# Scores from two of three half-precision products, and three weight blocks loaded and summed earlier

## The reference

```
style = s @ aff_w.T + aff_b ; w_mod = w * style ; w_mod *= rsqrt(sum(w_mod^2) + eps)
kx = x @ w_mod.T + b                      # per batch element, then 16 heads of 32
A  = softmax(kx[h] . kx[j] / sqrt(32))    # per token, 16 x 16 over its heads
x  = x + modulated_linear(A @ kx)
h = ln(ln(x, pathway), compartment); t = ln(x, time); s = ln(x, scale)
m, n, r = x + _mlp_ln(memory), x + _mlp_ln(noise), x + _mlp_ln(resource)
x  = x + ln(silu(cat(w0 h, w1 t, w2 m, w3 n, w4 r, w5 s) @ W1 + b1) @ W2 + b2)
```

## Time and profile before

| | |
|---|---|
| time, median of 3 | 870.54 us (870.13 to 871.36) |
| the profiled execution: its own time | 869.47 us |
| its span, first to last instruction | 867.6 us |
| PE busy | 836.8 us (96%) |
| DVE busy | 646.7 us (75%) |
| POOL busy | 605.7 us (70%) |
| ACT busy | 487.6 us (56%) |
| mean granted clock of PE | 0.989 of full speed |

### The profile page before, as it was taken

How to read it: one execution, slowest core, us unless ns; L and a number is a source line. 1 busy time by engine, 2 the same in 40 slices (tenths; PEclk the granted TensorE clock), 3 DMA queues, 4 the chain that set the end, 5 groups by cost and what they waited for, 6 DMA issues and landing times.

```text
span 867.6 us, 19685 instructions
## 1 busy us (share of the span) xinstructions
PE 836.8 (96%) x7456; PEld 731.9 (84%) x7474; DVE 646.7 (75%) x1067; ACT 487.6 (56%) x851; POOL 605.7 (70%) x766
## 2 busy tenths in 40 slices
PE   5996999999999999999999999999999999999997
PEld 5853888988889898888989898888988898898986
DVE  3589778778786867678797877679797767677652
ACT  3567555565656465465656556465647546464531
POOL 2367998778786767768776866668787775756472
PEclk9998999999999999999999999999999999999999
DMA  8972233424343333525243332424343342323110
GB/s 277 419 268 62 71 91 105 126 63 150 83 151 81 98 93 86 128 51 158 71 149 89 107 93 69 127 68 145 83 123 91 87 117 49 104 68 83 47 50 25
DMA packets 104365, 95.55 MB, mean 110 GB/s; under 512 B 72880, under 2 KB 78160, under 8 KB 102608
## 3 DMA queue, kind: packets, MB, share of 16 engines
q1 hardware_dynamic: 95056, 69.26, 27.7%
q0 software_dynamic: 4608, 16.78, 7.1%
q10 hardware_dynamic: 4608, 8.25, 2.8%
HBM read 69.60 MB, written 8.40 MB: 90 GB/s over the span
## 4 chain that ended last, share of the span: by engine, by line
PE 88%; DVE 5%; DMA 2%; POOL 2%; issue 1%; ACT 1%; ACTq 0%; another core or an unknown queue 0%; DVEq 0%; POOLq 0%
PE acc L405 43%; PE tok L405 28%; PE att L405 8%; PE xp L558 6%; PE xp L405 3%; DMA kb<-in_kb 1%; DVE stg_e L1284 1%; DMA pgb<-in_pw,pidx 1%; DVE raw_k L1170 0%; DVE W1xl L1274 0%; POOL op0l L1706 0%; DVE qt L1290 0%; POOL W2l L1710 0%; DVE q L1297 0%; DVE BD L1185 0%
## 5 line engine op out<-in xcount | busy, mean ns | idle before, releaser
L1706 POOL TENSOR_TENSOR op1l<-ytmp,op1h 128x512 fp32r<-128x512 f32 x64 | 89.8, 1403 | 20.1 <-ACT op1h L912 19.6
L1652 POOL TENSOR_TENSOR xlo<-xraw,xhi 128x512 fp32r<-128x512 f32 x31 | 40.5, 1306 | 68.0 <-ACT xhi L804 68.0
L405 PE MATMUL acc<-op0h,W1xh 128*128 128x256 f32 x256 | 75.8, 296 | 1.4 <-DVE op0l L1376 1.1
L405 PE MATMUL acc<-op1h,W1th 128*128 128x256 f32 x256 | 75.0, 293 | 0.0
L405 PE MATMUL acc<-op1h,W1hh 128*128 128x256 f32 x256 | 73.7, 288 | 0.0
L405 PE MATMUL acc<-op0h,W1sh 128*128 128x256 f32 x256 | 73.7, 288 | 0.0
L405 PE MATMUL acc<-op1h,W1tl 128*128 128x256 f32 x256 | 72.4, 283 | 0.0
L405 PE MATMUL acc<-op1l,W1hh 128*128 128x256 f32 x256 | 72.4, 283 | 0.0
L405 PE MATMUL acc<-op1l,W1th 128*128 128x256 f32 x256 | 72.4, 283 | 0.0
L405 PE MATMUL acc<-op0h,W1sl 128*128 128x256 f32 x256 | 72.4, 283 | 0.0
L405 PE MATMUL acc<-op1h,W1hl 128*128 128x256 f32 x256 | 72.4, 283 | 0.0
(11 more groups left out here) (269 smaller groups left out, 3005.2 us busy)
## 6 DMA issues: line engine op xcount, KB each, us to landing
xsq<-in_x SPq DMA_DIRECT2D x32, 256.0 KB, 3.1
xb<-in_x SPq DMA_DIRECT2D x32, 256.0 KB, 3.0
out<-xb SPq DMA_DIRECT2D x32, 256.0 KB, 2.4
BD<-q SPq DMA_DIRECT2D x124, 64.0 KB, 2.1
BD<-v SPq DMA_DIRECT2D x124, 64.0 KB
xraw<-in_xT SPq DMA_DIRECT2D x30, 256.0 KB, 3.0
ring<-in_k_wT ACTq DMA_DIRECT2D x6, 256.0 KB, 3.3
dmb<-dm_rows SPq DMA_DIRECT2D x6, 256.0 KB, 3.9
```

Source lines behind the costliest of these rows:

```text
L405: return e.matmul(o, a, b, start=start, stop=True, skip_group_check=True)
L1652: e.tensor_tensor(xlo[:, :, :], (xraw1 if g == 1 else xraw)[:, :, :], xhi[:, :, :].bitcast(F32), ALU.subtract).then_inc(s["xlo"], 1)
L1706: e.tensor_tensor(op[slot]["l"][:, :, half(g)], four(ytmp[YT[n, g][0]]), op[slot]["h"][:, :, half(g)].bitcast(F32), ALU.subtract).then_inc ...
```

## The change

Two things are changed, and a few instructions are placed elsewhere to suit.

First, `scores` leaves out the 32-column matmul (lo weights against hi). By the symmetry of the scores that product is the transpose of the hi.lo product that stands in `SE`. So `score_sum` now makes the transpose of `SE` in 32 x 32 blocks into `ET`, adds `SE` to the hi half, and after that adds `ET`.

Second, in the prologue, the blocks m and n (`raw["x"]`, `stg["a"]`) are loaded right after `o_wT` and r a little later, the blocks t, s, h after the second mlp weights. `mlp1` gets a buffer of its own and runs between `proj(0)` and `demodulation(1)`. `x_scaled`, the Silu of the mlps and `gain_tables` stand ahead of `score_low(0)` on ACT, and `x_weights` stands around `score_sum(0)` on DVE. `tables_tsh` is split, `vec_T` and `tables_mnr` come ahead of `proj(2)`, and `q_hi(2)`, `e_first(1)` stand behind the casts of W1's t block on ACT.

```
             e.dma_start(raw["o"][:, :, :], A["o_wT"]).then_inc(s["c_wo"], 16)
+            e.dma_start(raw["x"][:, :, :], A["int_w1"][2]).then_inc(s["c_rm"], 16)
+            e.dma_start(stg["a"][:, :, :], A["int_w1"][3]).then_inc(s["c_rn"], 16)
             load_sq(1)
-            e.dma_start(stg["a"][:, :, :], A["mlp1"]).then_inc(s["c_m1"], 16)
+            e.dma_start(mlp_w1[:, :, :], A["mlp1"]).then_inc(s["c_m1"], 16)
+            e.dma_start(raw["r"][:, :, :], A["int_w1"][4]).then_inc(s["c_rr"], 16)
...
-                    mm(both, diag(j, 0), q, start=(j % 8 == 0))
-                    i = mm(both[:, :, 0], diag(j, 1), q[:, :, 0])
+                    i = mm(both, diag(j, 0), q, start=(j % 8 == 0))
...
             proj(0)
+            mlp1()
             demodulation(1)
             scores(0)
             proj(1)
             mod_rows(1)
-            mlp1()
-            tables_tsh()
+            mlp2()
+            demod_T()
+            tables_tsh((0,))
             values(0)
-            demod_T()
-            mlp2()
+            tables_tsh((1, 2))
             a_T(0)
             scores(1)
+            tables_tsh((3,))
+            vec_T()
             out_proj(0)
+            tables_mnr()
             proj(2)
-            vec_T()
-            tables_mnr()
             values(1)
...
                 e.wait_ge(s["Sc"], 2 * g + 2)
-                e.tensor_tensor(high, high, SE[:, :], ALU.add).then_inc(s["Ss"], 1)
+                if g:
+                    e.wait_ge(s["aTr"], g)
+                e.transpose(ET[:, :], SE[:, :]).then_inc(s["lT"], 1)
+                e.tensor_tensor(high, high, SE[:, :], ALU.add).then_inc(s["lT"], 1)
+                e.wait_ge(s["lT"], 2 * g + 2)
+                e.tensor_tensor(high, high, ET[:, :], ALU.add).then_inc(s["Ss"], 1)
...
             w_T(0)
+            hidden_add()
             demod_eps(1)
+            x_weights(1, (0, 1))
             score_sum(0)
             less_max(0)
+            x_weights(1, (2, 3))
+            x_weights(2, (0, 1))
             q_lo(1)
             e_T(0)
             q_T(1)
             e_second(0)
-            hidden_add()
+            vectors()
             mod_first(1, range(4))
```

More of the change, by code:

```diff
@@ L136, in build @@
         raw["o"] = raw_o
+        mlp_w1 = at("mlp_w1", [128, 4, 512], offset=place["W2l"])
         stg = {n: at(f"stg_{n}", [128, 4, 512], offset=place[f"W{w}h"]) for n, w in zip("abcde", ("1x", "1t", "1s", "1h", "2"))}
@@ L331, in _ @@
             e.dma_start(raw["o"][:, :, :], A["o_wT"]).then_inc(s["c_wo"], 16)
+            e.dma_start(raw["x"][:, :, :], A["int_w1"][2]).then_inc(s["c_rm"], 16)
+            e.dma_start(stg["a"][:, :, :], A["int_w1"][3]).then_inc(s["c_rn"], 16)
             load_sq(1)
[L333 removed]
+            e.dma_start(mlp_w1[:, :, :], A["mlp1"]).then_inc(s["c_m1"], 16)
+            e.dma_start(raw["r"][:, :, :], A["int_w1"][4]).then_inc(s["c_rr"], 16)
             for i, n in enumerate(("mem", "noi", "res")):
                 e.dma_start(stg["bcd"[i]][:, :, :], A[n + "_w2"]).then_inc(s["c_w2"], 16)
[L336 removed]
+            e.wait_ge(s["tq"], 1)
+            for i in range(3):
+                e.dma_start(rv[i][:, :], A["rows_v"][i]).then_inc(s["c_rv"], 16)
             e.dma_start(raw["t"][:, :, :], A["int_w1"][1]).then_inc(s["c_rt"], 16)
@@ L462, in mlp1 @@
                         for c in cs:
-                            ins = mm(mlp[:, i * 16 + kt * 4:i * 16 + kt * 4 + 4], stg["a"][:, c, kt * 128:kt * 128 + 128], condT[:, c, :], start=(i == 0 and kt == 0 and c == 0))
+                            ins = mm(mlp[:, i * 16 + kt * 4:i * 16 + kt * 4 + 4], mlp_w1[:, c, kt * 128:kt * 128 + 128], condT[:, c, :], start=(i == 0 and kt == 0 and c == 0))
                 ins.then_inc(s["m1"], 1)
@@ L487, in tables_tsh @@
                     e.wait_ge(s["c_r" + n], 16)
-                for kt in range(4):
+                for kt in kts:
                     for n, quarter in (("t", 0), ("s", 1), ("h", 3)):
@@ L989, in _ @@
             q_hi(0)
+            x_scaled()
             split_x(1)
             squares(1)
+            e.wait_ge(s["mh"], 1)
+            e.activation(hT[:, :, :, 0:4].rearrange("p k i b -> p i k b"), hT[:, :, :, 0:4].rearrange("p k i b -> p i k b"), ACT.Silu).then_inc(s["hs"], 1)
+            gain_tables()
             score_low(0)
@@ L1015, in _ @@
                 j.then_inc(s["LB"], 1)
-            q_hi(2)
-            e_first(1)
             e.wait_ge(s["m2"], 3)
@@ L1020, in _ @@
             split_hi(W1["t", "h"], raw["t"], s["wh"])
+            q_hi(2)
+            e_first(1)
             z_make(0)
@@ L1036, in _ @@
                 e.wait_ge(s["xc"], kt + 3)
-                e.copy(W1["x", "h"][:, kt, :], stg["e"][:, kt, :]).then_inc(s["wh"], 1)
+                e.copy(W1["x", "h"][:, kt, :], stg["e"][:, kt, :]).then_inc(s["whx"], 1)
             x1_hi(0)
+            e.wait_ge(s["c_rh"], 16)
+            split_hi(W1["h", "h"], raw["h"], s["wh"])
             x1_hi(1)
@@ L1460, in _ @@
             a_sum(0)
-            vectors()
+            vectors_norm()
             a_lo(0)
+            vectors_end()
             score_sum(1)
             less_max(1)
-            vectors_norm()
-            vectors_end()
-            x_weights(1, (0,))
+            x_weights(2, (2, 3))
             e_T(1)
@@ L1473, in _ @@
             a_sum(1)
-            x_weights(1, (1, 2))
             a_lo(1)
-            x_weights(1, (3,))
             v_stats(0)
-            x_weights(2, (0, 1, 2))
             product(0, "t")
-            x_weights(2, (3,))
             w_T(2)
@@ L1731, in _ @@
             demod(1, 1)
+            e.wait_ge(s["h2"], 3)
+            e.tensor_tensor(small[0:96, 74:75], small[0:96, 73:74], eps5[0:96, :], ALU.add).then_inc(s["lnB"], 1)
+            e.wait_ge(s["lnB"], 1)
+            e.tensor_tensor(small[0:96, 75:76], small[0:96, 74:75], mh[0:96, :], ALU.pow).then_inc(s["lnB"], 1)
             for kt in range(4):
@@ L1735, in _ @@
             bounds(2)
-            e.wait_ge(s["h2"], 3)
-            e.tensor_tensor(small[0:96, 74:75], small[0:96, 73:74], eps5[0:96, :], ALU.add).then_inc(s["lnB"], 1)
-            e.wait_ge(s["lnB"], 1)
-            e.tensor_tensor(small[0:96, 75:76], small[0:96, 74:75], mh[0:96, :], ALU.pow).then_inc(s["lnB"], 1)
             add_ob(0)
@@ L1742, in _ @@
             add_ob(1)
+            e.wait_ge(s["wh"], 1)
+            e.wait_ge(s["Pm"], 3)
+            split_lo(W1["t", "l"], raw["t"], W1["t", "h"], None, (0, 1))
             root1(0)
```

37 lines of the change are left out of this document (12 added, 25 removed).

## The result

The changed kernel takes 890.83 us (median of 5 runs, 888.52 to 895.34) against 870.54 (median of 5). The ratio is 1.0235, with a 95% interval of 1.020 to 1.0269. The profiled execution was the longest of its five, 895.34 us, with a span of 893.5.

The account below looks back on a forecast made before the run. PE was taken to bound the loop, with DVE almost as late between `W2_part(pa)` and `x_T(pb)`. From 869.47 us profiled, loop +11.5 and prologue +4.5 gave 885.5; the median, 1.07 above the profiled execution, 886.5; range 866 to 896.

Parts of the forecast that it names:

- `x_one(b)` pushes `x_T(pb)`: Second half of passes 1 to 14: DVE's queue grows 1.36 us, 0.23 idle absorbs some, `x_T(pb)` comes 1.13 later.
- All of that keeps its distance to `x_T(pb)`, so it delays nothing more: Second half of a pass: work queued behind `score_sum`, `root1(b)` on POOL and both `x1_hi` on ACT add no delay.
- The loop's sum: Whole loop: 14 passes +8.4 us, six passes with weights +2.5, the end +0.6, in all +11.5.
- Item (1): Prologue: `mlp1`, 3.63 us, goes ahead of `scores(0)`, where PE waited 1.30 us: +2.3.
- Item (2): Prologue: two longer `score_sum` in the chain up to the exponential of group 1: +2.7 us.
- Item (3): Prologue, from the exponential of group 1 to `values(1)`: everything in a row, 9.0 us against 6.8 now, +2.3.
- Item (4): Prologue, `values(1)` to `x_T(1)`, 18.0 us now: of 7.4 us taken off DVE, 2.8 returned; the weakest term.
- The DMA order itself costs nothing I can find: Prologue loads: m and n fill a queue pause; t, s, h land some 2 us later but are needed later.
- A: Rival, at `x_T(pb)`: DVE work is hidden, PE 17.1 us faster, prologue neutral, 853.4 us; chance 0.12.
- C: Rival: loop loses about half, each `x_T(pb)` wait 0.8 us, a pass changes by -0.26; 867 to 871 us; chance 0.13.
- B: Rival: loop as forecast, prologue pays in full with -6 us, 876 us; chance 0.12.
- D: Rival: clock falls, each new wait in the loop brings 3.4 us at half clock, +24, 910 us; chance 0.05.

Follow-up runs that it names:

- e2: Changed kernel with the old scores and old `score_sum` put back, so the new prologue alone; 878.62 us, ratio 1.0072 to the kernel before.
- e5: e1 with `last_stats(pb)` on DVE moved behind `x1_lo` in the next pass; 881.14 us, ratio 1.0119 to the kernel before.
- e10: e5 with `exponential(a + 2)` on ACT moved behind both `x1_hi`; 874.09 us, ratio 1.0045 to the kernel before.
- e1: Kernel before with the score change alone, loads and order of the prologue as before; 881.35 us, ratio 1.0113.
- e11: Kernel before without the 16 lo.hi matmuls a group, DVE's added work done on other data ahead of `score_sum(b)`; 876.96 us, ratio 1.007.
- e8: e2 with the mlps' path put back (`mlp1`, `mlp2`, tables, Silu, `hidden_add`, vectors); 877.8 us, ratio 1.0085 to the kernel before.
- e9: e8 with `vec_T`, `tables_mnr` back behind `proj(2)`, and `q_hi(2)`, `e_first(1)` ahead of the t casts; 876.5 us, ratio 1.0067 to the kernel before.

## Why the prediction was right, and where it wasn't

The time, 890.83, is 4.3 us above the 886.5 predicted, inside 866 to 896, and the direction was given 0.72. The main step, the wait before `x_T(pb)`, was right. That the sum came this close is in part luck: terms of the loop balance each other, and the prologue's was too small. Of the signs named, the 14 waits, the pass (49.84, 49.9 said) and the transpose came; the wait itself is 0.98 us and not 1.5 to 1.8, and `x_T(1)` stands at 102.69 (97.39 in e2) and not near 92.5. By its own steps:

- **Price of the removal**: right. 16 matmuls of scores now take 0.56 and 0.52 us where 32 took 1.09, so 33 to 35 ns each as before.
- **Price of the addition**: 1.33 us in place of 1.36 (352.44 to 354.47 is 2.03 for what took 0.70); of it the transpose is 0.59 from start to start.
- **`x_one(b)` pushes `x_T(pb)`**: right in place and count, a quarter too large in size. 14 waits released by DVE xb; from DVE's start behind `W2_part(pa)` to `x_T(pb)` 7.38 us (350.03 to 357.41), 6.52 before, so 0.86 more where I had 1.13. Half of that difference is in the 0.19 us from the end of `xb` to `x_T(pb)`, which I took as fixed: it is 0.06 in the changed kernel (357.35 to 357.41), so 0.13 of it was slack. The wait of 1.66 that I announced before `x_T(pb)` is 1.14 by the distance of the two transposes; some 0.28 of the rest is a new wait of `out_proj(b)` for `alo`, which now comes sooner after the shorter scores.
- **"All of that keeps its distance to `x_T(pb)`, so it delays nothing more"**: wrong, and hidden by the step before. The exponential in ACT's queue ahead of `x1_hi` was a second bound of the same size (e5, e10). The sum is the same with it, since in the changed kernel the exponential ends at 357.66 and the late `x_T(pb)` only at 358.07, so ACT's queue adds next to nothing; whoever had acted on my text and cleared DVE's queue would have gained nothing.
- **The loop's sum**: +11.5 said, +11.2 measured. Its terms balance each other. A pass without weights costs 0.53 and not 0.60. The six passes with weights cost some 0.7 more than that in all and not 2.5, and the pass behind the last of them 0.3 more. The end costs 0.8 and not 0.6. And passes 1 and 2 cost 3.1 us together and not 1.2, of which a stretch at half clock from 143.7 to 147.1 us is a part.
- **The prologue**: the term that was wrong, +4.5 said, +14.65 in the profiled execution, 7.4 by e2's median. Item (1), `mlp1` ahead of `scores(0)`, was +2.3 and is +7.7 at `scores(0)`: I had priced the 32 matmuls at the clock of their old place and not looked at what then falls on the stretch of half clock. From 34.4 to 48.1 us PE is at half clock without an idle moment; it fell 2.3 us after the first of these matmuls, which have 4 columns each. `mlp1` takes 4.5 us (32.06 to 36.56) and `demodulation(1)` 6.8 (36.56 to 43.38); before, at full clock, `demodulation(1)` took 3.6 (30.73 to 35.67, less the wait of 1.30). Item (2), the longer `score_sum`, was +2.7 and is nothing (e1): ACT was late there and not DVE. The exponential then came 12.5 us later than before and not 5. Item (3), from the exponential to `values(1)`, was 9.0 and is 10.0 from its end, the best of the four. Item (4), from `values(1)` to `x_T(1)`, was 15.2 and is 17.0.
- **"The DMA order itself costs nothing I can find"**: not so at one place at least. DVE, before the modulation of the first weights:

```profile
24.30 0.26 DVE L1267 TENSOR_SCALAR Lt<-p_tabT,w 128x60 f32<-128x60 f32 x1 [6.31 <-DMA pidx<-in_pidx]
```

 The small load pidx is issued from ACT's queue, where the change has nothing, and landed at 24.28, 18.69 before, while the two 1 MB blocks that now follow `o_wT` on SP's queue were under way (they landed at 21.97 and 24.70). The first modulation starts 1.0 us later for it (24.79, 23.79 before), and 0.2 later in e2, where pidx is late by 4.7. So it is a small part of the 7 to 15 us. The block t, said to land some 2 us later, lands 6.6 later (44.68 us, 38.07 before), but its first matmul starts at 55.7. What the order costs in all was not run apart.
- **Rivals**: A fell at once, with more waits in the loop and not fewer. C fell with the price of the DVE instructions. B had its sign wrong: the prologue alone is slower by 7.4 (e2). D's falling clock in the loop came once, for 3.4 us, but half clock did lengthen the prologue, where I had not asked about it.

## What to carry to other kernels

When one result is late at a consumer, follow what else hangs on the same chain through every engine's queue before moving anything: here two queues carried the same delay to PE, and the profile names only the first. A removal is worth its own length only where the engine isn't handed its work by another one; price it stretch by stretch. In a prologue where each engine waits for the next in turn, putting one step back moves the wait to the next step, so its gain has to be read at the end and not at its own place.

## What I had not expected of the hardware

- DVE's addition with two operands in SBUF took 2.07 us when a POOL instruction of 1.31 that reads SBUF ran beside it, and 0.69 alone (e11), as if the whole of POOL's instruction had been waited for. The Trainium skill, SBUF — State Buffer, section Who interferes with whom, has DVE and GpSimd share a port pair under an exclusive lock; the trace agrees in the length of the delay. By the trace DVE's instruction started 0.21 us before POOL's, so it doesn't show which of the two had the ports first. The additions of the change itself have one operand in PSUM and took 0.66 to 0.70 in all 32 groups.
- The load of ACT's table for the exponential, 1.28 us, is hidden when the exponential waits for its input anyway, and comes into the open when it is moved behind (e10: 342.33, then the exponential at 343.62). The Trainium skill, ScalarE: Activation LUTs, section What ACT_TABLE_LOAD costs, adds a drain of about 1380 ns; between these two rows there is none.
- A small load issued by one engine came later when another engine issued large loads: pidx landed between 18.2 and 18.9 us in the ten profiled executions with the old order of loads and between 22.9 and 24.3 in the four with two 1 MB blocks more ahead (after, e2, e8, e9). The 16 DMA engines had a share of 1.02 of their time from 20 to 30 us in either order (before and after).
